# A gated delta-rule attention layer with a column-routed feed-forward: tile products in whole batches, and a new order of the work on all engines

## The chip, the cores and the metric

The kernel runs on one core of a Trainium2 chip. The time is the device time of one execution in microseconds; lower is better. The core has five engines that run side by side and meet at semaphores: PE (TensorE, matrix products, with PEld for its weight loads), DVE (VectorE), ACT (ScalarE), POOL (GpSimd) and SP (SyncE, which here issues the DMAs).

## The reference, cut to what matters

All is in fp32; x is 4 sequences of 2048 tokens of 512 numbers, 16 heads of 32.

```
q, k, v, gate = x@Wq.T, x@Wk.T, x@Wv.T, x@Wg.T      # heads of 32; x is layer-normed before
beta  = sigmoid(x@Wb.T)
alpha = exp(-exp(A_log) * softplus(x@Wa.T + dt_bias))
q = q/|q|/sqrt(32);  k = k/|k|
for each token t:                                   # S: 32x32 per sequence and head
    S = S*alpha_t
    delta = (v_t - k_t.S) * beta_t
    S = S + k_t (x) delta
    y_t = q_t.S
x1 = x + layernorm( (rmsnorm(y)*silu(gate)) @ Wo.T + bo )
xf = layernorm(x1)
logits = cos(xf, col_emb) + sigmoid(gelu(xf@gate_w1 + b1)@gate_w2 + b2)     # 16 columns
e = argmax(logits);  w = softmax(logits)[e]
out = x1 + layernorm( LN( (w*gelu(xf@W_cols[e] + b_cols[e])) @ proj_w[e] + proj_b + xf ) )
```

## The kernel before, in words

The recurrence is done in chunks of 32 tokens. A step handles a block of 64 tokens of all four sequences (256 tokens), in two chunks c = 0, 1. There are 32 blocks. Four stages of different blocks run side by side in one step, and `step` of each engine says with flags which of them are there: `ahead` (block b: norm, transposes, projections to q, k, gate, beta, v, decays), `chain` (block b-1: the recurrence), `after` (block b-2: output norm, output projection, residual, norm of x1, hidden layer of the gate), `late` (block b-3: logits, choice of the column, the scatter of rows by column). So there are 35 steps, 29 of them with all four stages. Behind them comes a second part over the columns' rows, which the change leaves as it is.

Each engine has one order of work, written out by hand in its `step`; an engine does its work in that order and waits in place. Heads lie as 16 groups g of 4 heads on the 128 partitions. What a head does alone is a product on a 32x32 tile of the array; `on_tiles(half, ...)` (lines 456 to 463) issues 8 groups times 4 heads of them. A batch is both halves, 64 products, which the trace shows as 128 records. They are, per chunk c:

- `key_products(c)` (L469): keys with keys and queries, into `kkq`
- `state_to_u(c)` (L477): keys with the state S, into `uk`
- `first_half_to_u(c)` (L485): the correction of a chunk's second half by its first
- `state_to_outputs(c)` (L492) and `chunk_to_outputs(c)` (L497): outputs, into `uq`
- `change_state(c)` (L504): into `su`, which `add_to_state` (DVE, L1165) adds to S

In the kernel before, most batches are issued in halves with large 128x128 products between them: `project` (L437, half of one projection, 8 records), `squares_sum` (L446), `output_projection` (L535), `gate_hidden` (L543), `gate_logits` (L553), `log_alpha` (L511), `decays` (L522) and the transposes `turn` (L454). Three PSUM banks (`work0` to `work2`) serve all these in the order of the list TURNS; `into` waits until the bank's last user was read.

DVE solves each chunk in two halves by forward substitution: `solve_half(c, j)` (L1145 to L1160), 15 rounds of four operations and a transpose. Its factors `pairs` are written to DRAM and fetched back by SP as rows broadcast over partitions (`write_rows`, `fetch_pairs`), and multiplied by beta on POOL (L992). ACT copies out of PSUM and evaluates functions; logarithm and exponential, sigmoid, and gelu lie in different tables, and a change of table is a table load in its stream. `token_norm` (L771 to L774) gives the scale of a layer norm, `norm_tokens` (L752) applies it, `length_of_normed` (L781 to L786) gives the length of the normed rows.

Of the kernel before, what the change touches and what calls it, by code (L numbers as in the profile page):

```python
# [16 lines left out]
H, DH = 16, 32  # L17
# [37 lines left out]
    ("logits",), ("xT", 0), ("xT", 1), ("qk", 0), ("rms", 0), ("rms", 1), ("alpha",), ("qk", 1), ("ss", 0),  # L55
    ("qk", 2), ("wo", 0), ("wo", 1), ("rank",), ("ss", 1), ("G", 0), ("G", 1), ("qk", 3), ("ss", 2),
    ("gate", 0), ("ss", 3), ("gate", 1), ("beta", 0), ("beta", 1), ("xfT", 0), ("xfT", 1), ("v", 0), ("v", 1),
    ("hid",),
]
BANK = {use: n % NW for n, use in enumerate(TURNS)}  # L60
READ_BY = dict(xT="xT_ready", qk="q_sq_ready", ss="ss_read", alpha="alpha_read", rms="rms_read", G="eg_ready", wo="wo_read",
               rank="rank_read", gate="gate_used", beta="beta_ready", v="v_read", xfT="xfT_ready", hid="h_ready",
# [26 lines left out]
def sandwich_kernel(nc, x, w_in, wa, dt_bias, a_log, norm_w, wo, bo, col_emb, gw1, gb1, gw2, gb2,  # L89
                    w_cols, b_cols, proj_w, proj_b, ln_g, ln_b,  # L90
                    c_sq, c_sel, c_mask, c_iota, c_pad, c_tok, c_row, c_col, out, xs_dram):
    with ExitStack() as ctx:
# [34 lines left out]
        minus_half = sb("minus_half", [P, 1])  # L127
# [17 lines left out]
        qraw = [sb(f"qraw{n}", [P, GU * T]) for n in range(2)]  # L145
        qsq = [sb(f"qsq{n}", [P, GU * T]) for n in range(2)]
        qr = [sb(f"qr{n}", [P, GU * T]) for n in range(2)]
        sg = sb("sg", [P, GU * T])
# [36 lines left out]
        gsb = qsq[1][:], ctx_flat[:, 0:GU * T]  # L185
        gT = qraw[1][:], ctx_flat[:, GU * T:2 * GU * T]
# [35 lines left out]
        def in_qr(*shape, dt=F32):  # L222
# [37 lines left out]
            v_full beta_full gate_full v_read beta_ready vb_free gate_ready gate_used  # L260
# [55 lines left out]
        def _(sp):  # L316
# [44 lines left out]
            def step(chain, after, ahead, block, following):  # L361
# [5 lines left out]
                if chain:  # L367
                    write_rows(1)
                    fetch_pairs(1, 0)
                    fetch_pairs(1, 1)  # L370
                if ahead:
                    load_tokens(following)
                    write_rows(0)
                if after:
                    store(block)
                if ahead:
                    fetch_pairs(0, 0)
# [41 lines left out]
        def _(pe):  # L419
# [45 lines left out]
            def key_products(c, half):  # L465

                if not half:
                    take(pe, "A_ready", free=1, use="kkq")
                on_tiles(half, "kkq_full", lambda g, q, q_half: pe.matmul(  # L469
                    kkq[q, g], kq[q, g, c, 0, :], kq[q, g, c].rearrange("p a t -> p (a t)"), start=True, stop=True))  # L470

            def state_to_u(c, half):

                if not half:
                    take(pe, "kqd_ready")
                    take(pe, "S_ready")
                on_tiles(half, "uk_full", lambda g, q, q_half: pe.matmul(  # L477
                    uk[q, g], S[q, g, :], kqd[c][q, g, 0, :], start=(g == 0), stop=True, skip_group_check=True))

            def first_half_to_u(c, half):  # L480

                if not half:
                    take(pe, "A_ready")
                    take(pe, "delT_ready")
                on_tiles(half, "corr_full", lambda g, q, q_half: pe.matmul(  # L485
                    uk[q, g, CS:C], delT[c][q_half, g, :], Ak[c][q_half, 1, g, :],
                    start=False, stop=True, skip_group_check=True))

            def state_to_outputs(c, half):
                if not half:  # L490
                    take(pe, "uq_free", free=1)
                on_tiles(half, None, lambda g, q, q_half: pe.matmul(  # L492
# [959 lines left out]
```

## Time and profile before

| | us |
|---|---|
| three runs | 3433.52 median (3429.26 to 3442.22) |
| profiled execution, its own time | 3454.87 |
| its span, first to last instruction | 3453.1 |
| mean granted TensorE clock, of full | 0.912 |
| the 35 steps, from the start to about | 3072 |
| ACT busy, of the span | 1824.4 |
| DVE busy | 2357.6 |
| POOL busy | 1913.1 |
| DMA, mean share of 16 engines | 0.42 + 0.05 + 0.01 by queue |

Busy time of one engine overlaps that of the others; matmul records overlap each other as well, so differences between starts are safer than durations. The second part over the columns takes the last 380 us or so of the span. An engine's idle time is shown with who ended it; "issue" is a wait for which the profile shows no releaser.

### The profile page before, as it was taken

How to read it: one execution, taken by the hardware profiler on the slowest of the kernel's cores; microseconds unless marked ns; L12 is line 12 of the kernel's file. 1: busy time of each engine (PE TensorE's matmuls, PEld its weight loads, DVE VectorE, ACT ScalarE, POOL GpSimd, SP SyncE). 2: the span in 40 equal slices, each digit the busy share in tenths (PEclk: the TensorE clock that was granted, in tenths of full speed). 3: DMA queues.
4: the chain of work that ended last, by engine and by line, in shares of the span. 5: the costliest groups of instructions: out<-in, count | busy, mean ns of one | idle time of the engine just before them, and what ended most of it. 6: DMA issues, size and time to landing. Idle time of an engine off the chain costs nothing.

```text
span 3453.1 us, 141658 instructions
## 1 busy us (share of the span) xinstructions
PE 3006.9 (87%) x59368; PEld 2295.4 (66%) x59368; DVE 2357.6 (68%) x10708; ACT 1824.4 (53%) x4154; POOL 1913.1 (55%) x2903
## 2 busy tenths in 40 slices
PE   4899999999999999999999999999999999637774
PEld 4667777777777777777777777777777777414443
DVE  1667666666666766777666666666666677657896
ACT  2355555555555555555555555555555555326664
POOL 1555565455555555555565555555556555416887
PEclk9899999999999999999999999999999999759997
DMA  3544444544444445444444454444445444545773
GB/s 112 132 119 115 113 117 112 124 117 108 118 115 114 117 121 124 112 113 117 115 117 112 124 124 110 114 115 115 116 116 124 124 111 118 142 141 105 132 126 65
DMA packets 350030, 404.87 MB, mean 117 GB/s; under 512 B 31169, under 2 KB 293953, under 8 KB 348881
## 3 DMA queue, kind: packets, MB, share of 16 engines
q1 hardware_dynamic: 332752, 362.10, 42.1%
q0 software_dynamic: 16640, 33.71, 5.4%
q8 instruction: 468, 7.67, 1.0%
q14 instruction: 170, 1.38, 0.1%
HBM read 323.97 MB, written 75.93 MB: 116 GB/s over the span
## 4 chain that ended last, share of the span: by engine, by line
PE 62%; ACT 20%; DVE 11%; issue 4%; POOL 1%; ACTq 1%; DMA 1%; POOLq 0%; SPq 0%; DVEq 0%
PE work L437 25%; PE work L535 7%; PE work L543 3%; PE work L446 3%; DVE uk L1158 3%; DVE Ut L1155 3%; PE su L504 3%; PE work L454 2%; PE uq L497 2%; PE uk L477 2%; PE kkq L469 2%; PE uq L492 2%; PE work L530 2%; PE work L522 2%; PE work L511 2%
## 5 line engine op out<-in xcount | busy, mean ns | idle before, releaser
L437 PE MATMUL work<-xT,w_sb 128*128 128x256 f32 x5120 | 1314.1, 407 | 6.5 <-ACT beta L835 5.1
L992 POOL TENSOR_TENSOR pairs<-pairs,beta 128x240 f32<-128x240 f32 (+14 forms) x1920 | 862.4, 488 | 667.0 <-ACT beta L835 380.9
L437 PEld LDWEIGHTS work<-xT,w_sb 128*128 128x128 f32 x5120 | 996.3, 202 | 183.8 <-issue 31.1
L1158 DVE TENSOR_TENSOR uk<-uk,Ut 128x120 f32<-128x120 f32 (+14 forms) x3840 | 708.6, 226 | 1.1
L1155 DVE TENSOR_TENSOR Ut<-pairs,uk 128x120 f32<-128x120 f32 (+14 forms) x3840 | 688.2, 215 | 5.5 <-POOL pairs L992 5.0
L802 ACT ACTIVATE qraw<-work 128x512 f32<-128x512 f32 x128 | 75.9, 593 | 432.2 <-DVE kq L1171 305.5
L1165 DVE TENSOR_TENSOR S<-Sd,su 128x512 f32<-128x512 f32 x64 | 44.0, 687 | 359.1 <-PE su L504 359.1
L535 PE MATMUL work<-wo_sb,ctxT 128*128 128x512 f32 x512 | 240.6, 613 | 6.3 <-POOL ctxT L1011 6.3
L1003 POOL TENSOR_TENSOR kd<-kd,dec 128x512 f32<-128x512 f32 x64 | 68.0, 1084 | 258.8 <-DVE kd L1237 258.8
L492 PEld LDWEIGHTS uq<-kqd,S 32*32 32x32 f32 x8192 | 90.7, 114 | 156.8 <-ACT oT L792 105.8
L1145 DVE TENSOR_TENSOR uk<-vT,uk 128x128 f32<-128x128 f32 x256 | 62.9, 291 | 187.7 <-PE uk L485 115.8
L492 PE MATMUL uq<-kqd,S 32*32 32x32 f32 x8192 | 105.6, 203 | 95.7 <-ACT oT L792 93.4
L809 ACT ACTIVATE qr<-work 128x512 f32<-128x512 f32 x128 | 75.9, 593 | 193.9 <-PE work L446 191.5
L1017 POOL TENSOR_TENSOR xfw<-xfw,pb_sb 128x1024 f32<-128x1024 f32 x32 | 75.5, 2359 | 175.7 <-DVE slot L1224 175.7
L535 PEld LDWEIGHTS work<-wo_sb,ctxT 128*128 128x128 f32 x512 | 93.7, 193 | 105.4 <-issue 94.8
L1171 DVE TENSOR_TENSOR kq<-qraw,qr 128x512 f32<-128x512 f32 x128 | 136.1, 1082 | 35.0 <-ACT qr L810 35.0
L839 ACT ACTIVATE vT<-work 128x512 f32<-128x512 f32 x64 | 38.2, 597 | 224.5 <-PE work L437 224.5
L981 POOL TENSOR_TENSOR kqd<-kq,eg 128x1024 f32<-128x1024 f32 x64 | 150.3, 2349 | 3.8 <-DVE kq L1171 3.8
L976 POOL TENSOR_TENSOR Sd<-S,eg_end 128x512 f32<-128x512 f32 x64 | 67.9, 1061 | 148.6 <-DVE S L1165 148.6
L446 PE MATMUL work<-qsq,squares 128*128 128x512 f32 x256 | 147.0, 658 | 0.0
L469 PEld LDWEIGHTS kkq<-kq 32*32 32x32 f32 x8192 | 119.1, 105 | 34.1 <-issue 29.8
L1194 DVE TENSOR_TENSOR lt<-work,gb_sb 128x32 f32<-128x32 f32 x32 | 6.1, 191 | 195.7 <-PE work L556 195.7
(249 smaller groups left out, 5970.8 us busy)
## 6 DMA issues: line engine op xcount, KB each, us to landing
pairs<-pair_rows SPq DMA_DIRECT2D x512, 256.0 KB, 3.5
pairs<-pair_rows SPq DMA_DIRECT2D x512, 224.0 KB, 3.7
xt<-in_x SPq DMA_DIRECT2D x66, 256.0 KB, 5.4
pair_rows<-Ak SPq DMA_DIRECT2D x64, 256.0 KB, 2.3
x<-in_x SPq DMA_DIRECT2D x64, 256.0 KB, 4.8
out<-x SPq DMA_DIRECT2D x64, 256.0 KB, 3.7
wo_sb<-xs_rows SPq DMA_DIRECT2D x30, 258.0 KB, 2.9
w_sb<-in_w_in SPq DMA_DIRECT2D x1, 5120.0 KB, 14.9
```

The source lines that it names most:

```text
L437: mm = pe.matmul(w[:, half * BT:(half + 1) * BT], w_sb[:, f, j * D + hg * P:j * D + (hg + 1) * P], xT[:, f, :], start=(f == 0), stop=(f == ...
L446: pe.matmul(w, blk1, qsq[n % 2][:], start=True, stop=True).then_inc(s["ss_full"], 1)
L469: on_tiles(half, "kkq_full", lambda g, q, q_half: pe.matmul(kkq[q, g], kq[q, g, c, 0, :], kq[q, g, c].rearrange("p a t -> p (a t)"), start ...
L492: on_tiles(half, None, lambda g, q, q_half: pe.matmul(uq[q, g], S[q, g, :], kqd[c][q, g, 1, :], start=(g == 0), stop=True, skip_group_chec ...
L504: on_tiles(half, "su_full", lambda g, q, q_half: pe.matmul(su[q, g, :], kd[c][q, g, :], delT[c][q, g, :], start=True, stop=True))
L535: mm = pe.matmul(w, flat(ctxT[:, hg * B + tb * BL:hg * B + (tb + 1) * BL, :]), wo_sb[:, hg, :], start=(hg == 0), stop=(hg == KD - 1))
L543: mm = pe.matmul(w[:, n * BT:(n + 1) * BT], gw1_sb[:, f, n * P:(n + 1) * P], xfT[:, f, :], start=(f == 0), stop=(f == KD - 1))
L981: link(nc.gpsimd.tensor_tensor(kqd[c][:], kq[:, :, c], eg[:, :, c * C:(c + 1) * C].unsqueeze(2).to_broadcast([P, G, 2, C]), ALU.mult), "kq ...
L992: ins = nc.gpsimd.tensor_tensor(a, a, beta[:, :, t:t + WID[t0]], ALU.mult)
L1155: link(v.tensor_tensor(Ut[:, g, 0:n], pr[:, g], uk[:, g, at:at + 1].to_broadcast([P, G // 2, n]), ALU.mult), "vb_free" if i and (c, j, t0) ...
L1158: link(v.tensor_tensor(uk[:, g, at + 1:at + 1 + n], uk[:, g, at + 1:at + 1 + n], Ut[:, g, 0:n], ALU.subtract), f"pairs_free{j}" if i and t ...
L1171: link(v.tensor_tensor(unit(kq, hp)[:, :, :, 1 - j, :], per_chunk(qraw[n % 2][:]), per_chunk(qr[n % 2][:]), ALU.mult), "kq_ready", hold=(n ...
```

## The change: what it does

- TensorE: `on_tiles` issues a whole batch, and the batches stand together where they did not: `state_to_u(0)`, `key_products(1)`, `state_to_outputs(0)` at the start of a step; `chunk_to_outputs(0)`, `state_to_u(1)`, `state_to_outputs(1)` behind `change_state(0)` and `output_projection(1)`; `first_half_to_u(1)` before `key_products(0)`. `change_state(1)` comes before two halves of v, `chunk_to_outputs(1)` and `gate_hidden`, in the step itself and not in the next one. TURNS has another order, and alpha's numbers share a bank with the logits.
- ScalarE: q and k are copied straight to `kq` (and scaled in place by DVE), the decays straight to `dec`. Sigmoid of beta is tanh and a linear step; the gate is copied, and its tanh is taken later; DVE's `gate_values` makes gate*(1+tanh(gate/2)), and the factor one half goes into `nw`. Both tanh come behind one table load with gelu, and `length_of_normed` moves to the next step. The output copy of chunk 0 stands before the norm of y, that of chunk 1 behind gelu.
- VectorE: another order; `output_rows` of both halves before `add_to_state`, the statistics of y behind the ranks; `decay_products(0)` inside `solve_half(1, 1)`; `vb_free` is signalled at that solve's start.
- GpSimd: decay differences before the scatter, `decay_state(1)` and the first part of `pairs_times_beta(1, 1)` before the residual sum.
- SP: `load_tokens` before `fetch_pairs(1, 1)`, `store` before `write_rows(0)`.

The diff's core:

```diff
-            def on_tiles(half, full, product):
-                for g in range(half * GU, (half + 1) * GU):
+            def on_tiles(product):
+                for g in range(G):
                     for h in range(HP):
                         mm = product(g, slice(DH * h, DH * h + DH), slice(DH * h, DH * h + CS))
-                if half and full:
-                    mm.then_inc(s[full], 1)
+                return mm
...
# TensorE, the new step
                 if chain:
+                    state_to_u(0)
+                    key_products(1)
+                    state_to_outputs(0)
                 if ahead:
                     take(pe, "xn_ready", TB)
                     turn("xT", xn, 0)
                     turn("xT", xn, 1)
                 if after:
                     outputs_squares_sum(0)
                     outputs_squares_sum(1)
                 if ahead:
                     take(pe, "xT_ready", 2)
                     project("qk", 0, 0, 0)
+                if late:
+                    gate_logits(0)
+                if ahead:
                     project("qk", 0, 0, 1)
+                if late:
+                    gate_logits(1)
+                if ahead:
+                    log_alpha(0, late)
+                    log_alpha(1, late)
                     project("qk", 0, 1, 0)
+                    project("qk", 0, 1, 1)
+                if chain:
+                    first_half_to_u(0)
+                if ahead:
                     squares_sum(0)
                     project("qk", 1, 0, 0)
                     project("qk", 1, 0, 1)
                     squares_sum(1)
                     take(pe, "lax_ready")
                     decays(0)
                     decays(1)
+                if after:
+                    take(pe, "ctx_ready", 2)
+                    output_projection(0)
+                if chain:
+                    change_state(0)
+                if after:
+                    output_projection(1)
+                if chain:
+                    chunk_to_outputs(0)
+                    state_to_u(1)
+                    state_to_outputs(1)
+                if late:
+                    ranks()
+                if ahead:
+                    squares_sum(2)
                     project("qk", 1, 1, 0)
                     project("qk", 1, 1, 1)
                     project("gate", 4, 0, 0)
+                    project("gate", 4, 0, 1)
                     squares_sum(3)
                     project("gate", 4, 1, 0)
                     project("gate", 4, 1, 1)
+                if chain:
+                    first_half_to_u(1)
+                if ahead:
                     take(pe, "kq_ready", 4)
+                    key_products(0)
                     project("beta", 3, 0, 0)
                     project("beta", 3, 0, 1)
                     project("beta", 3, 1, 0)
+                    project("beta", 3, 1, 1)
                 if after:
                     take(pe, "xf_ready", TB)
                     turn("xfT", xfw, 0)
                     turn("xfT", xfw, 1)
                 if ahead:
                     project("v", 2, 0, 0)
                     project("v", 2, 0, 1)
+                if chain:
+                    change_state(1)
+                if ahead:
                     project("v", 2, 1, 0)
+                    project("v", 2, 1, 1)
+                if chain:
+                    chunk_to_outputs(1)
                 if after:
                     take(pe, "xfT_ready", 2)
                     gate_hidden()
...
# ScalarE, new helpers and the new step's second half
+            def copy_gate(p, hp):
+                take(act, "gate_full")
+                link(nc.scalar.activation(flat(unit(silu[1 - p], hp)), bank("gate", hp), ACT.Copy), "gate_read", hold=True)
+            def gate_tanh(p, hp):
+                nc.scalar.activation(gate_t[hp], flat(unit(silu[1 - p], hp)), ACT.Tanh, scale=0.5).then_inc(s["gate_ready"], 1)
+            def beta_sigmoid(hp):
+                b = flat(unit(beta, hp))
+                take(act, "beta_full")
+                link(nc.scalar.activation(b, bank("beta", hp), ACT.Tanh, scale=0.5), "beta_read", hold=True)
+                link(nc.scalar.activation(b, b, ACT.Identity, scale=0.5, bias=half[:]), "beta_ready")
...
+                if after:
+                    take(act, "ctx_raw", 2)
+                if chain:
+                    copy_outputs(0)
+                if ahead:
+                    inverse_norm(2)
+                    copy_and_square(3)
                 if after:
                     take(act, "y_mv_ready")
                     token_norm(y_rn, y_mv)
                     norm_tokens(y, y, y_rn, "zn_ready")
                 if ahead:
                     pair_decays(0)
                     pair_decays(1)
+                    copy_gate(p, 0)
                     inverse_norm(3)
+                    copy_gate(p, 1)
                 if after:
                     take(act, "x1_mv_ready")
                     token_norm(x1_rn, x1_mv)
                     norm_tokens(xfw, x1, x1_rn, "xf_ready")
+                if ahead:
+                    take(act, "x_mv_ready")
+                    token_norm(x_rn, x_mv)
+                load_tanh_gelu()
                 if ahead:
                     if chain:
                         take(act, "vb_free")
+                        take(act, "pr_ready", 8)
+                    beta_sigmoid(0)
+                    beta_sigmoid(1)
+                    gate_tanh(p, 0)
+                    gate_tanh(p, 1)
...
# VectorE, the new step from the first correction on
                 if chain:
                     take(dve, "corr_full")
                     solve_half(0, 1)
+                if ahead:
+                    scale(0)
                 if late:
                     choose_columns()
+                if after:
+                    output_rows(0)
+                    output_rows(1)
+                if chain:
+                    add_to_state()
+                if ahead:
+                    for hp in range(2):
+                        take(dve, "g_copied")
+                        link(v.transpose(gT[hp], flat(unit(dec, hp))), "gT_ready")
                 if late:
                     weigh_columns()
                     rows_of_tokens()
+                if after:
+                    for tb in range(TB):
+                        token_stats(y, y_mv, tb, "y_mv_ready")
                 if ahead:
                     scale(1)
                 if chain:
                     take(dve, "uk_full")
                     solve_half(1, 0)
                 if ahead:
                     scale(2)
                     scale(3)
                 if after:
                     for tb in range(TB):
                         take(dve, "x1_ready")
                         token_stats(x1, x1_mv, tb, "x1_mv_ready")
                 if ahead:
+                    next_tokens_stats()
                     take(dve, "dec_ready", 2)
+                if chain:
+                    take(dve, "corr_full")
+                    solve_half(1, 1, {2: lambda: decay_products(0)} if ahead else {})
+                if ahead:
+                    gate_values(p, 0)
+                    gate_values(p, 1)
+                if chain:
+                    add_to_state()
```

## Rows read from the trace of the kernel before

**Rows 1.** The page: the span, TensorE's busy time, the queue that carries instructions.

```profile
span 3453.1 us, 141658 instructions
...
PE 3006.9 (87%) x59368; PEld 2295.4 (66%) x59368; DVE 2357.6 (68%) x10708; ACT 1824.4 (53%) x4154; POOL 1913.1 (55%) x2903
...
q8 instruction: 468, 7.67, 1.0%
```

**Rows 2.** TensorE in time: start, us, line, operation, records [idle before, who ended it].

```profile
56.32 5.34 PE L437 MATMUL work<-xT,w_sb 128*128 128x256 f32 x24
61.50 1.02 PE L446 MATMUL work<-qsq,squares 128*128 128x512 f32 x2
...
125.76 1.29 PE L504 MATMUL su<-delT,kd 32*32 32x32 f32 x128 [3.29 <-DVE delT L1160]
...
1408.99 0.75 PE L504 MATMUL su<-delT,kd 32*32 32x32 f32 x64
...
1435.91 1.99 PE L437 MATMUL work<-xT,w_sb 128*128 128x256 f32 x8
1437.84 1.10 PE L469 MATMUL kkq<-kq 32*32 32x64 f32 x64
...
1501.25 0.75 PE L504 MATMUL su<-delT,kd 32*32 32x32 f32 x64
```

**Rows 3.** TensorE's idle moments of one step; one row of the waits over the span.

```profile
1421.24 0.24 PE L477 MATMUL uk<-kqd,S 32*32 32x32 f32 x3 [0.35 <-issue]
1422.25 0.40 PE L477 MATMUL uk<-kqd,S 32*32 32x32 f32 x19 [0.76 <-issue]
...
1449.36 1.08 PE L492 MATMUL uq<-kqd,S 32*32 32x32 f32 x64 [2.94 <-ACT oT L792]
1451.90 1.12 PE L454 MATMUL work<-squares,xfw 128*128 128x128 f32 x4 [1.46 <-ACT beta L835]
...
1472.12 1.75 PE L454 MATMUL work<-squares,xn 128*128 128x128 f32 x8 [0.65 <-ACT xn L752]
...
PE uk L477 <- issue: 26.0, 52, 1.7
```

**Rows 4.** ScalarE in time, the same step.

```profile
1443.99 1.28 ACT L785 ACT_TABLE_LOAD   x1
...
1449.95 1.28 ACT L835 ACT_TABLE_LOAD   x1
...
1467.75 0.29 ACT L771 ACTIVATE nsc<-x_mv,eps 128x2 f32<-128x2 f32 x1
...
1470.55 1.52 ACT L752 ACTIVATE xn<-xt,x_rn 128x512 f32<-128x512 f32 x2
```

**Rows 5.** VectorE in time: a half solve's ends, a row of the ranks, scales, statistics.

```profile
1398.55 0.49 DVE L1145 TENSOR_TENSOR uk<-vT,uk 128x128 f32<-128x128 f32 x2 [1.27 <-PE uk L485]
...
1407.81 0.72 DVE L1160 STREAM_TRANSPOSE delT<-uk 128x512 f32<-128x512 f32 x1
...
1415.59 0.16 DVE L1219 TENSOR_TENSOR lt<-work,rows 128x32 f32<-128x32 f32 x1
...
1432.60 1.74 DVE L1171 TENSOR_TENSOR kq<-qraw,qr 128x512 f32<-128x512 f32 x2
...
1434.86 0.68 DVE L1121 BATCH_NORM_STATS2 stats<-x 128x6 f32<-128x512 f32 x1
```

**Rows 6.** Busy time by stretch, then granted clock, DMA share, GB/s; two projection rows.

```profile
1449.40:1456.00 6.60, 5.14 (x89) 4.15 (x93) 4.79 (x35) 2.90 (x4) 3.59 (x7) 0.55 0.72 139
1472.10:1476.00 3.90, 3.88 (x137) 3.49 (x138) 3.90 (x23) 1.51 (x4) 3.84 (x11) 0.56 0.18 40
1485.60:1489.80 4.20, 4.20 (x12) 2.80 (x11) 1.99 (x5) 0.69 (x3) 2.90 (x3) 0.59 0.71 130
...
1452.81 3.14 PE L437 MATMUL work<-xT,w_sb 128*128 128x256 f32 x8
...
1485.57 3.31 PE L437 MATMUL work<-xT,w_sb 128*128 128x256 f32 x8
```

More of the change, by code:

```diff
@@ L489, in state_to_outputs @@
[L489 to L492, printed above, removed]
-                    uq[q, g], S[q, g, :], kqd[c][q, g, 1, :], start=(g == 0), stop=True, skip_group_check=True))
-            def chunk_to_outputs(c, half):
-                on_tiles(half, "o_full", lambda g, q, q_half: pe.matmul(
-                    uq[q, g], delT[c][q, g, :], Aq[c][q, g, :], start=False, stop=True, skip_group_check=True))
@@ L500, in change_state, with key_products @@
-            def change_state(c, half):
-                if not half:
-                    take(pe, "delT_ready")
-                    take(pe, "kd_ready")
-                on_tiles(half, "su_full", lambda g, q, q_half: pe.matmul(
-                    su[q, g, :], kd[c][q, g, :], delT[c][q, g, :], start=True, stop=True))
-            def log_alpha(tb):
-                w = bank("alpha") if tb else into("alpha")
+                return mm
+            def key_products(c):
+                take(pe, "A_ready", free=1, use="kkq")
+                on_tiles(lambda g, q, q_half: pe.matmul(
+                    kkq[q, g], kq[q, g, c, 0, :], kq[q, g, c].rearrange("p a t -> p (a t)"), start=True, stop=True))\
+                    .then_inc(s["kkq_full"], 1)
@@ L510, in log_alpha, with change_state @@
+            def change_state(c):
+                take(pe, "delT_ready")
+                take(pe, "kd_ready")
+                on_tiles(lambda g, q, q_half: pe.matmul(
+                    su[q, g, :], kd[c][q, g, :], delT[c][q, g, :], start=True, stop=True)).then_inc(s["su_full"], 1)
+            def log_alpha(tb, late):
+                w = bank("alpha") if tb or late else into("alpha")
+                at = 2 * TB * E + tb * H
                 for f in range(KD):
-                    mm = pe.matmul(w[:, tb * H:(tb + 1) * H], xT[:, f, tb * P:(tb + 1) * P], wa_sb[:, f, :],
+                    mm = pe.matmul(w[:, at:at + H], xT[:, f, tb * P:(tb + 1) * P], wa_sb[:, f, :],
@@ L670, in step @@
                     turn("xfT", xfw, 0)
-                if ahead:
-                    project("beta", 3, 1, 1)
-                if chain:
-                    state_to_outputs(1, 0)
-                if after:
                     turn("xfT", xfw, 1)
@@ L1155, in solve_half @@
                         link(v.tensor_tensor(Ut[:, g, 0:n], pr[:, g], uk[:, g, at:at + 1].to_broadcast([P, G // 2, n]), ALU.mult),
[L1156 removed]
+                             behind=1)
                     for i, g in enumerate(turns):
@@ L1279, in step @@
                     scale(3)
-                    take(dve, "gate_ready")
-                    link(v.tensor_tensor(flat(unit(silu[1 - p], 0)), bank("gate", 0), sg[:], ALU.mult), "gate_used")
                 if after:
```

290 lines of the change are left out of this document (104 added, 186 removed).

## The prediction

> **What bounds the kernel now.** First the page's shares: TensorE is busy 87% of the span and leads the list; the reader is to see that nothing else comes near [rows 1]. Then TensorE's instructions in order of time, to find the period of the loop: the same batch of the state's change starts at 1408.99 and at 1501.25, so a step takes 92.26 us, and 32 such steps make about 2950 of the 3453 us [rows 2]. The kernel's time is therefore the step's time, and the step is read from TensorE: what it works on, where it stands idle, and where its clock is low.
>
> Idle in this step: 0.35 + 0.76 (inside state_to_u(1), no releaser shown), 2.94 (state_to_outputs(1) for ScalarE's copy of uq), 1.46 (xfT for the bank that beta's sigmoid reads) and 0.65 us (xT for xn), together 6.16 us [rows 3]. The two long ones have one cause in ScalarE's order: between 1435.6 and 1451.9 it runs the norm of x1, the length of the normed rows and the sigmoid in one string, with five table loads of 1.28 us in it, two of them shown [rows 4], while TensorE waits behind that string.
>
> Low clock in this step: three stretches of 6.6, 3.9 and 4.2 us with a granted mean of 0.55, 0.56 and 0.59, the rest at 1.0 (2.4 GHz); as the mean of a stretch mixes the two levels, twice what is missing to 1.0 makes 12.7 us at the lower one, 1.2 GHz [rows 6]. In them a projection half takes 3.14 and 3.31 us against 1.99 [rows 2, 6]; adding the same differences for the transposes and tile batches that lie there gives about 4.3 us lost. The first stretch follows the long idle time; the other two follow stretches of tile batches and narrow products with hardly an idle moment.
>
> So a step is 92.26 = 6.16 idle + 4.3 low clock + 81.8 of TensorE work at full clock.
>
> **The change part by part.**
>
> 1. Whole batches. A half batch of 32x32 products takes 0.75 us, a whole one 1.29, both with the same overlap of some 0.06 into the next row (1435.91 + 1.99 against 1437.84) [rows 2]. So a half costs 0.54, and each entry into tiles 0.15. The large products around pay too: a projection half among its like takes (61.50 - 56.32)/3 = 1.73 us, between tile batches 1.93, so 0.20 per group of tiles [rows 2]. I take 0.33 a group (both together, rounded down). Before, a full step has 22 groups of tiles separated by large products; after, 7: state_to_u(0) with key_products(1) and state_to_outputs(0); the first correction; the first state's change; chunk_to_outputs(0) with state_to_u(1) and state_to_outputs(1); the second correction with key_products(0); the second state's change; chunk_to_outputs(1). 15 fewer at 0.33 are -4.95 us. The arithmetic is unchanged. Ends: if only the switch inside the tiles counts, -2.2; if the large products' whole 0.20 counts, -5.3.
>
> 2. ScalarE's tables. Sigmoid becomes tanh with a linear step, in one set with gelu; the length of the normed rows moves to the next step's front, where logarithm and exponential are loaded. Eight loads a step become two, if tanh lies in gelu's set; if not, one more. At 1.28 us a load, six are 7.7 us of ScalarE, and two copies of the gate and two linear steps for beta (0.6 each, as the copies there) are 2.4 back. ScalarE has slack, so only its strings count. The Trainium skill (ScalarE: Activation LUTs, What ACT_TABLE_LOAD costs) gives about 2.66 us for a switch of set, 1.38 of it a drain after the load. The trace disagrees: the load at 1443.99 is followed at once by the next operations. By the page ScalarE would be freed of 16 us instead of 7.7; the sum here would be the same, since what is left of its strings is short.
>
> 3. The old idle times. The output copy stands now early in ScalarE's order, before y's norm: the 2.94 goes. 1.46 and 0.65 change their form and are counted anew below. So -6.16, and everything that is late next is added.
>
> 4. What is late next: a walk through the new order with the durations of rows 2, 4 and 5 at full clock, from state_to_u(0) at 0.
> - xn: gelu, the output copy, one table load and norm_tokens (1.52 [rows 4]) end at about 4.4; the three tile batches end at 4.1. 0.3 to 0.4.
> - solve(0,1) takes 9.97 us (1398.55 to the end of the transpose at 1408.53 [rows 5]) and starts at 20.8; the state's change comes at 31. No wait, but nothing to spare.
> - The product between the state's change and the next chunk: add_to_state now stands behind output_rows(1), which needs output_projection(1). It ends at 36.0, S is there at 37.5, and chunk_to_outputs(0) covers 36.0 to 37.2. 0.3.
> - The second correction: after ranks TensorE has six projection halves and two sums of squares, 12.2 us; VectorE has in the same time five small operations (0.16 to 0.2 each), statistics of y (two at 0.68 and an aggregate of 0.2 each), one scale (0.87) and solve(1,0) (9.97), 13.5 us [rows 5]. Wait 1.3 to 1.4.
> - key_products(0) needs scale(2) and (3), 1.74 us after that solve [rows 5], with a correction of 1.2 in between: 0.5.
> - xfT's second turn needs the bank read by beta's tanh: statistics of x1 and of the next tokens 3.5, x1's norm 2.8 + 1.5 (1467.75 to the end of 1470.55's two), the tokens' norm 2.8, a load 1.28 and the tanh 0.6 stand against key_products and beta's four halves: 1.4. Then v waits 0.5 for the second tanh.
> - solve(1,1), with decay_products in it, ends at 71.3; the state's change comes at 72. After it come v's last two halves, chunk_to_outputs(1) and gate_hidden, 8.5 us, which cover S for the next step.
> Sum 4.3 us of new waits (rounding included). Everything queued behind such a wait on TensorE is delayed with it, and ScalarE and VectorE follow.
> GpSimd and the queue of SP: fetch_pairs(1,1) is now behind load_tokens, which waits for eg; the walk has its data 3 us or more before GpSimd reaches them, and the other three fetches earlier still. This is hidden; if the cover went, it would cost what the fetch is late, 1 to 3 us. Waits on the buffers (kd, kqd, kt, gate_used) are added, all satisfied 2 us or more before. Bounds of the new waits: 0.8 (only those without chain) to 8.
>
> 5. Supply of instructions. The idle moments with no releaser are 26.0 us in 52 times at state_to_u over the span, the longest 1.7 [rows 3]; all instructions come by a queue of 7.67 MB [rows 1]. They fall in a stretch of tiles. I keep them at 1.4 a step with longer stretches of tiles (bounds 0 to 5).
>
> 6. Clock. The two low stretches that follow narrow work stay; the one after the long idle time should shrink, but three tile batches in a row are new. I take 3.8 us of loss instead of 4.3 (bounds 0.5 to 12).
>
> Sum: 81.8 - 4.95 + 4.3 + 1.4 + 3.8 = 86.35 us a step, 5.9 less. Times 31 (thirty full steps and two partial ones) -183, and 5 less at the closing steps, where table loads of x1's norm lie on the path. The profiled execution took 3454.87 us and would take 3267; the median of the three runs is 21 below it, so 3433.5 - 188 = **3245 us**. The later part over the columns isn't touched.
>
> **The rivals.**
> - A, the clock stays up: loss 0.5 instead of 3.8, a step of 83.05, 3433.5 - 286 - 5 = 3143. For it: the longest idle time left is 1.4 us. Against: two of three low stretches came without idle time.
> - B, tiles in a row outrun their instructions: each of the three long groups of tiles stalls by 1.4 instead of one, +2.8, a step of 89.2, 3334. For it: the stalls lie in tiles, and with up to 192 small products in a row there has been no row. Against: a batch of 128 records ran in 1.29 at 125.76 without one.
> - C, slower: the low clock takes over. Place: the groups of three batches at the step's start and in its middle, each with waits near it (xn, S, the second correction). Price: 3.31 against 1.99 is 0.4 to 0.45 us per us at the lower level. It decides from about 22 us low in a step (granted mean under 0.88 against 0.93), where the loss reaches 9.7 and eats the 5.9; at 28 us a step is 95, 3433.5 + 85 = about 3520. The Trainium skill (TensorE: Matmul & The Clock Gate, A second HAM failure mode) says that frequent short idle moments between groups of products bring the clock down again and again; that would speak for C. The trace bears it out in part only: the stalls of 0.35 and 0.76 left the clock at 1.0, the 2.94 did not.
> - D, no change: the new waits reach their bound of 8 and B's stalls come on top, +6.5 on the forecast, a step of 92.85, 3433.5 + 18 - 5 = 3447, within 17 us of before. For it: the walk has several places with nothing to spare. Against: both must come at once.
>
> **How the numbers follow.** The forecast has 0.64 (its own range 3190 to 3300), A 0.12, B 0.10, C 0.10, D 0.04. 0.5% of 3433 is 17 us, about what a measurement can tell from none. Faster: forecast, A and B, 0.86; the same 0.04; slower 0.10. The range reaches from A's time to a little over B's, 3140 to 3350, and leaves out C and D and the tail beyond A.
>
> **What would show it.** A step's period near 86 with 7 groups of tiles at 1.2 to 1.3 us a batch and projection halves at 1.73 (1); two table loads a step (2); no idle at state_to_outputs(1) for ScalarE (3); idle before first_half_to_u(1), xfT and v of 1 to 1.5 us, VectorE or ScalarE named (4); idle without releaser inside the long groups (5, B); the granted clock by stretches (6, A, C). It is wrong if one of the new waits is over 4 us, if the step's granted mean leaves 0.90 to 0.96, or if a batch in a row takes over 1.5 us.

## The result, and the profile after

The changed kernel takes 3638.5 us (median of 4 runs, 3623.8 to 3656.2) against 3435.9 for the kernel before in the same comparison: a ratio of 1.059, 95% interval 1.054 to 1.065. It is slower by 203 us; the forecast was 3245.

The page after, the same lines as in [rows 1], and the granted clock by slices:

```profile
span 3641.3 us, 141487 instructions
...
PE 2997.7 (82%) x59368; PEld 2372.4 (65%) x59368; DVE 2353.2 (65%) x10710; ACT 1654.4 (45%) x4103; POOL 1912.2 (53%) x2903
...
PEclk9889889889988889898898898889988998668898
...
q8 instruction: 468, 7.67, 0.9%
```

TensorE has the same number of records and nearly the same busy time, and a longer span: it waits more. For whom, its waits over the span say (engine, line, waited for: us, times, longest):

```profile
PE uq L488 <- issue: 138.5, 64, 4.4
PE kkq L465 <- issue: 122.9, 59, 3.4
PE uk L473 <- issue: 88.7, 39, 4.1
```

All three large ones have no releaser (I call such a wait a stall), and nearly all of them stand at the second and third batch of a group: state_to_outputs, key_products, state_to_u. The engines' waits that the prediction walked through are nearly gone.

Counting over whole steps makes the comparison exact. Stretches of whole steps, from one ranks product to another of a later step (columns as in [rows 6]), before:

```profile
486.65:2796.70 2310.05, 2156.02 (x45509) 1669.21 (x45501) 1593.35 (x7877) 1262.52 (x2800) 1291.23 (x1950) 0.93 0.47 117
```

and after:

```profile
421.39:2778.06 2356.67, 2056.64 (x43685) 1656.60 (x43680) 1524.40 (x7560) 1071.34 (x2640) 1238.90 (x1872) 0.89 0.44 110
```

The first holds 25 steps, the second 24: a step takes 92.40 and 98.19 us. With TensorE's idle time in the same stretches from its waits, and the low clock as twice what the granted mean lacks to 1.0. The mean is printed with two digits, so each time at the low clock is known to about 1 us here; added up over 300 short windows it is 13.2 before and 22.0 after. The work is not measured: 76.85 is the forecast's own figure, and the loss is what it leaves over:

| a step, us | before | forecast | after |
|---|---|---|---|
| work at full clock (worked out) | 81.8 | 76.85 | 76.85 |
| stalls without releaser | 1.13 | 1.4 | 12.05 |
| waits for other engines | 5.02 | 4.3 | 0.45 |
| what is left: loss at the low clock | 4.4 | 3.8 | 8.8 |
| sum | 92.4 | 86.35 | 98.2 |
| of it, time at the low clock | 12.9 | | 21.6 |

8.8 of loss on 21.6 us is 0.41 us for each at the low clock, which fits the two projection halves of [rows 6] (3.31 against 1.99 us: 0.40); so the forecast's work for the kernel after stands, as an estimate. Before, 4.4 on 12.9 is only 0.34; at 0.40 the work there would be about 81.0, 0.8 less than the prediction took.

TensorE in time in the kernel after, the group of three at a step's start and the one in its middle (columns as in [rows 2]):

```profile
1548.55 0.83 PE L473 MATMUL uk<-kqd,S 32*32 32x32 f32 x76 [0.19 <-issue]
...
1549.23 0.91 PE L465 MATMUL kkq<-kq 32*32 32x64 f32 x48
1552.02 1.26 PE L465 MATMUL kkq<-kq 32*32 32x64 f32 x75 [1.87 <-issue]
...
1555.49 0.98 PE L488 MATMUL uq<-kqd,S 32*32 32x32 f32 x78 [1.71 <-issue]
...
1582.29 1.29 PE L501 MATMUL su<-delT,kd 32*32 32x32 f32 x128
...
1590.93 0.94 PE L473 MATMUL uk<-kqd,S 32*32 32x32 f32 x90 [1.55 <-issue]
...
1594.40 1.49 PE L488 MATMUL uq<-kqd,S 32*32 32x32 f32 x92 [2.17 <-issue]
```

Two things are to be seen. The stalls are in the middle of a batch, where no semaphore is waited for. And they stand 3.47 us apart (1548.55, 1552.02, 1555.49; 1590.93, 1594.40), with 128 records between them: 92 of state_to_u and 36 of state_to_outputs in the last pair (rows of one to three records, where two batches overlap, are left out above). The instruction queue tells what 128 records are. 7.67 MB for 2 x 59368 records (a product and its weight load each) is 64.6 bytes an instruction, so queue q8 carries TensorE's instructions and hardly any others, and 7.67 MB in 468 packets is 16.4 KB a packet. A packet then holds about 254 to 256 instructions: 128 records with their weight loads, exactly one batch of tiles.

What the stalls bring with them, by stretch behind the group in the middle (granted clock is the third number from the right):

```profile
1588.00:1592.00 4.00, 2.00 (x212) 1.80 (x198) 2.62 (x7) 0.60 (x1) 2.49 (x3) 1.00 0.54 119
1592.00:1596.00 4.00, 1.83 (x117) 1.65 (x104) 0.00 (x0) 0.00 (x0) 2.52 (x3) 0.55 0.50 139
1596.00:1600.00 4.00, 4.00 (x12) 2.88 (x13) 2.01 (x8) 0.30 (x1) 1.18 (x1) 0.50 0.59 131
```

TensorE is idle half of the first 8 us, and the granted clock falls from 1.00 to 0.50 for the ranks and the projections behind.

ScalarE's tables came as meant. The table loads in the whole program after, two a step and one for the second part, are 36 + 35 + 1; before, there were 251, eight in a full step:

```profile
L712 ACT ACT_TABLE_LOAD x36 | 46.2, 1283 | 31.1 <-DMA nw<-in_norm_w 30.4
L715 ACT ACT_TABLE_LOAD x35 | 44.9, 1283 | 0.7
L919 ACT ACT_TABLE_LOAD x1 | 1.3, 1283 | 0.0
```

### The profile page after: what moved, and what is told of

It reads as the page before. It is cut to its first block, busy times and chain, and to the rows that moved or that the text cites. A ratio compares the mean times of both kernels' runs of the same rounds, so it can differ in the third digit from the quotient of the medians.

```text
span 3641.3 us, 141487 instructions
## 1 busy us (share of the span) xinstructions
PE 2997.7 (82%) x59368; PEld 2372.4 (65%) x59368; DVE 2353.2 (65%) x10710; ACT 1654.4 (45%) x4103; POOL 1912.2 (53%) x2903
## 3 DMA queue, kind: packets, MB, share of 16 engines
q8 instruction: 468, 7.67, 0.9%
## 4 chain that ended last, share of the span: by engine, by line
PE 73%; issue 12%; DVE 8%; ACT 4%; POOL 1%; ACTq 1%; DMA 0%; DVEq 0%; POOLq 0%
PE work L435 30%; PE work L533 6%; PE kkq L465 4%; PE work L444 4%; PE work L541 3%; PE uq L488 3%; PE uk L473 2%; PE work L528 2%; PE work L452 2%; PE su L501 2%; PE uk L481 2%; PE uq L493 2%; PE work L509 2%; PE work L520 2%; PE work L551 1%
## 5 line engine op out<-in xcount | busy, mean ns | idle before, releaser
L435 PE MATMUL work<-xT,w_sb 128*128 128x256 f32 x5120 | 1254.4, 402 | 6.6 <-ACT beta L814 3.3
L435 PEld LDWEIGHTS work<-xT,w_sb 128*128 128x128 f32 x5120 | 1029.4, 204 | 243.9 <-issue 88.9
L465 PE MATMUL kkq<-kq 32*32 32x64 f32 x8192 | 175.2, 243 | 128.6 <-issue 122.9
L1007 POOL TENSOR_TENSOR dec<-dec,xn 128x512 f32<-128x512 f32 x64 | 81.8, 1278 | 326.5 <-DVE xn L1262 326.5
L465 PEld LDWEIGHTS kkq<-kq 32*32 32x32 f32 x8192 | 154.0, 123 | 140.5 <-issue 134.3
L488 PEld LDWEIGHTS uq<-kqd,S 32*32 32x32 f32 x8192 | 114.1, 134 | 143.8 <-issue 143.8
L770 ACT ACTIVATE kq<-work 128x512 f32<-128x512 f32 x128 | 75.8, 592 | 230.9 <-PE work L435 230.8
L473 PE MATMUL uk<-kqd,S 32*32 32x32 f32 x8192 | 95.4, 198 | 96.3 <-issue 88.7
L473 PEld LDWEIGHTS uk<-kqd,S 32*32 32x32 f32 x8192 | 84.4, 109 | 111.8 <-issue 111.4
L995 POOL COPY xt<-la 128x1024 f32<-128x1024 f32 x32 | 33.2, 1036 | 221.7 <-DVE la L1173 221.7
```

The lines of the kernel that those rows point to most:

```text
L435: mm = pe.matmul(w[:, half * BT:(half + 1) * BT], w_sb[:, f, j * D + hg * P:j * D + (hg + 1) * P], xT[:, f, :], start=(f == 0), stop=(f == ...
L465: on_tiles(lambda g, q, q_half: pe.matmul(kkq[q, g], kq[q, g, c, 0, :], kq[q, g, c].rearrange("p a t -> p (a t)"), start=True, stop=True))\
L473: on_tiles(lambda g, q, q_half: pe.matmul(uk[q, g], S[q, g, :], kqd[c][q, g, 0, :], start=(g == 0), stop=True, skip_group_check=True))\
L488: on_tiles(lambda g, q, q_half: pe.matmul(uq[q, g], S[q, g, :], kqd[c][q, g, 1, :], start=(g == 0), stop=True, skip_group_check=True))
L1007: link(nc.gpsimd.tensor_tensor(d, d, gT[hp], ALU.subtract))
```

## The experiments

Theory S, formed on the trace after: TensorE's instructions arrive in blocks of one batch at a pace of their own, and batches in a row outrun it. Rivals: W, the new order's own waits; T, tile products in a row are slow by themselves. All experiments give the reference's arithmetic but where the text says otherwise.

**e1_apart.** The kernel after, TensorE's `step` alone reordered so that no two batches stand together. In short form, with | between the parts (xT the transposes of xn, rms `outputs_squares_sum`, ss `squares_sum`, and qk, gate, beta halves of those projections):

```diff
-state_to_u(0) key_products(1) state_to_outputs(0) | xT | rms | qk
+state_to_u(0) | xT | key_products(1) | rms | qk | state_to_outputs(0)
-chunk_to_outputs(0) state_to_u(1) state_to_outputs(1) | ranks | ss 2 | qk, qk | gate
+chunk_to_outputs(0) | ranks | ss 2 | state_to_u(1) | qk, qk | state_to_outputs(1) | gate
-first_half_to_u(1) key_products(0) | beta
+first_half_to_u(1) | beta | key_products(0)
```

> The kernel after, with TensorE's order changed alone: whole batches stay, but no two stand side by side; key_products(1) behind the xT transposes, state_to_outputs(0) behind a projection half, state_to_u(1) behind ranks and a sum of squares, state_to_outputs(1) behind two projection halves, key_products(0) behind a half of beta. 12 groups of one batch instead of 7. Theory S (supply): TensorE's instructions come in blocks of 7.67 MB / 468 = 16.4 KB, 256 instructions of 64 bytes, as many as one batch has (128 products and 128 weight loads); a batch eats one in 1.3 us and the next isn't there. With large products between, the stalls without releaser, 11.9 us a step in the kernel after, fall to 1 to 3 us; a step of 98.1 goes to 87 to 90, 3290 to 3380 in all. Theory W (waits of the new order, VectorE's solves behind output_rows and ranks): stays at 97 to 99 a step, 3600 to 3650. Theory T (a change of kind of tile product, PSUM target or operand costs it, whatever stands between): every batch stalls still, no gain, 3600 or more.

Measured: 3375.9 us, ratio to before 0.982 (0.979 to 0.985). So 262 us, more than the whole slowdown, are undone by TensorE's order alone, and W and T fall. A step takes 89.58: stalls 3.14, waits for other engines 4.62, 7.2 us at the low clock. The waits:

```profile
PE work L452 <- ACT xn L726: 67.9, 25, 3.0
PE uk L473 <- issue: 36.7, 33, 2.3
PE uk L481 <- DVE delT L1156: 20.3, 17, 2.6
PE work L452 <- ACT beta L820: 16.5, 15, 2.2
```

The largest, 2.7 us a step for xn, belongs to e1's order and not to the forecast's walk:

```profile
2502.39 1.29 PE L473 MATMUL uk<-kqd,S 32*32 32x32 f32 x128
2506.71 1.97 PE L452 MATMUL work<-squares,xn 128*128 128x128 f32 x8 [3.04 <-ACT xn L726]
```

The transposes start 4.32 us after state_to_u(0), and the forecast had xn ready at 4.4; but e1 has one batch of 1.29 us in front of them, where the kernel after has three. In the kernel after xn is ready 4.27 us after state_to_u(0) (1551.99 on ScalarE) and the transposes come at 1556.40, since the stalls hold TensorE up that long. The other waits of e1 make 1.9 us a step, where the walk had 3.9.

**e4_front.** e1 with the first group in a row again.

> As e1, but with the first group of the kernel after kept: state_to_u(0), key_products(1), state_to_outputs(0) in a row at the step's start; everything else apart. Theory S: this group alone stalls 3.5 us a step as it does in the kernel after (1.9 and 1.7 in a step), and saves two switches: +2.8 to +3.5 us a step over e1, +90 to +110 in all, and the stalls stand inside the group's second and third batch, about 128 records after each other. Theory W: no difference from e1.

Measured: 3414.0 us, ratio 0.994 (0.992 to 0.996), 38 us over e1, where 90 to 110 was expected. Stalls rise from 3.14 to 7.02 a step, somewhat more than expected, but waits fall from 4.62 to 1.77: the stalls, and the two batches now there, stand in front of the wait for xn and take its place. The step is only 1.6 longer. A stall costs nothing where there would be a wait anyway.

**e2_halves.** The kernel after with every batch cut in halves, large products between.

> The kernel after, with TensorE's order changed alone: every batch is issued in two halves with a large product or transposes between, 21 to 22 groups a step as in the kernel before, all other engines as in the kernel after. Theory S: no stalls beyond the 1 to 1.5 us a step of the kernel before; against e1 it pays the switch in and out of tiles ten times more, 0.33 each, +3.3 us a step, +100 in all minus what e1 still stalls: 3350 to 3450. Theory W: as e1, no gain over the kernel after, 3600 or more. If the switch costs nothing, it is equal to e1 or faster.

Measured: 3576.5 us, ratio 1.043 (1.040 to 1.045). Stalls are 0.43 a step, fewer than anywhere, as S says. But the time is outside S's 3350 to 3450, and by the time alone W (3600 or more) is nearer; it is 200 over e1 where 100 was expected. A step is 95.88, 6.3 more than e1's: 2.7 less of stalls, 3.1 more of waits for other engines (7.73, most of it for VectorE's delT and ScalarE's xn; likely since the second halves stand behind more products, which no run takes apart), and 5.9 of work and low clock. By the short windows it has 7.2 us more at the low clock (14.0 against 6.9), about 2.9 at 0.40 each, so about 3.0 is left for nine or ten more groups of tiles, 0.3 each (an estimate).

**e3_before_whole.** The kernel before, each batch whole at its first half's place:

```diff
-                for g in range(half * GU, (half + 1) * GU):
+                if half:
+                    return
+                for g in range(G):
...
-                if half and full:
+                if full:
```

> The kernel before, with one edit: each batch is issued whole where its first half stood; the second half's place is empty. 12 groups instead of 22, none side by side. If whole batches save 0.33 each and single ones don't stall: -3.3 us a step, about -100, 3335. Theory S: small stalls may come where a batch meets few large products (chunk_to_outputs, one projection, key_products), up to 2 us a step, then -40 to -100. Theory T or a loss from whole batches as such: slower than before, 3450 to 3550.

Measured: 3418.0 us, ratio 0.995 (0.993 to 0.997). The gain is there, but it is 17 us, a sixth of what the switches promised and outside the 40 to 100 expected. A step is 90.83, 1.57 shorter: stalls 1.22 as before, waits 5.74 (+0.7), and 15.6 us at the low clock instead of 13.2 by the short windows, about 1 us of loss at 0.40. Ten groups fewer at 0.33 are -3.3, and the sum comes out at -1.5.

**e5_rows and e6_rows_traffic.** The kernel before with rows of products on constants ahead of its first step; in e6 with 80 transfers of 256 KB beside them, two at a time. In short form:

```diff
+            tiles(6, C, n32);  large(24)       # 6 batches in a row, 32 columns
+            tiles(6, 2 * C, n64);  large(24)   # 64 columns
+            tiles(6, P, n128);  large(24)      # 128 columns
+            for _ in range(6):
+                tiles(1, C, n32);  large(4)    # one batch, one projection half
+            for _ in range(6):
+                tiles(1, C, n32);  large(8)    # one batch, two halves
```

> The kernel before, with a stretch of products put ahead of its first step, whose results nobody reads, and no transfer running meanwhile: 6 batches of 32x32 products in a row with 32 columns; 6 with 64; 6 with 128; then 6 single batches of 32 columns with 4 large products (one projection half, 1.73 us) between; then 6 with 8 (3.46 us) between; 24 or 16 large products between these parts. Theory S: after one to three batches at 1.2 us the row runs at the pace of the blocks of instructions, one batch in 2.5 to 3.5 us, the same for 32 and 64 columns, with pauses each 128 records; single batches with one half between (3.0 us) run with small pauses or none, those with two (4.7 us) with none. Theory T (tiles slow by themselves in a row): pauses don't come each 128 records, and 64 columns take longer than 32 by their columns. If the supply suffers from transfers alone: no pause here at all.

> As e5, while the queue of SP runs 80 broadcast transfers of 256 KB, two outstanding, as for the pairs. If the blocks of instructions wait behind other transfers in the DMA engines: the pace of a row of batches goes from that of e5 to 3.5 us or more a batch. If the pace is the queue's own: the same as in e5 within 0.3 us.

TensorE in time in e5, no transfer running:

```profile
43.33 1.74 PE L710 MATMUL uk<-squares 32*32 32x32 f32 x183
47.49 1.27 PE L710 MATMUL uk<-squares 32*32 32x32 f32 x128 [2.43 <-issue]
51.23 1.93 PE L710 MATMUL uk<-squares 32*32 32x32 f32 x128 [2.46 <-issue]
...
80.59 1.99 PE L710 MATMUL kkq<-squares 32*32 32x64 f32 x128 [1.44 <-issue]
84.04 1.99 PE L710 MATMUL kkq<-squares 32*32 32x64 f32 x128 [1.47 <-issue]
...
103.72 16.57 PE L710 MATMUL work<-squares 32*32 32x128 f32 x599
120.58 5.11 PE L710 MATMUL work<-squares 32*32 32x128 f32 x169 [0.28 <-issue]
...
139.32 0.45 PE L710 MATMUL uk<-squares 32*32 32x32 f32 x31
140.03 1.02 PE L710 MATMUL uk<-squares 32*32 32x32 f32 x97 [0.27 <-issue]
...
175.66 1.29 PE L710 MATMUL uk<-squares 32*32 32x32 f32 x128
176.88 3.72 PE L715 MATMUL work<-w_sb 128*128 128x256 f32 x16
180.53 1.29 PE L710 MATMUL uk<-squares 32*32 32x32 f32 x128
```

Here is the cost by itself. In a row a batch comes each 3.73 us with 32 columns and each 3.45 to 3.73 with 64, with a pause at each 128 records, though 64 columns are twice as many: the pace is the instructions'. Meanwhile the core moves 4 GB/s (from 43 to 66 us), what one packet of 16.4 KB each 3.73 us makes (4.4), so the blocks are all that moves. A limit on single instructions would spread the pauses; here 128 records run through in 1.3 to 2 us and then the row stands still. The row starts with 183 records before its first pause, so what lay ready and came meanwhile is one block and a part. With 128 columns a batch is work for 3.5 us, and the one pause is 0.28. One batch with one projection half (1.73 us) between has pauses of 0.27 to 1.77 us; with two halves (3.46 us) none. T is refuted. Without transfers a batch of 1.29 us wants more than 1.73 us of other work, and 3.46 is enough; by the pace it would be about 2.4 (3.73 less 1.29, an estimate). S's own range for the pace, 2.5 to 3.5 us, was a little low.

The same row with transfers (e6):

```profile
50.73 1.93 PE L719 MATMUL uk<-squares 32*32 32x32 f32 x128 [3.94 <-issue]
55.56 1.93 PE L719 MATMUL uk<-squares 32*32 32x32 f32 x128 [2.91 <-issue]
61.75 1.93 PE L719 MATMUL uk<-squares 32*32 32x32 f32 x128 [4.27 <-issue]
```

The pace goes to 4.8 to 6.2 us a batch (the core moves about 195 GB/s, more than the 110 to 117 of the kernels' steps): the blocks come later beside other transfers. Here two halves between are not always enough either: the last batches pause for 0.18 to 1.27 us inside.

**e7_little_traffic.** The kernel after, each fetch of pairs cut to one row, so that its solves work on other numbers:

```diff
-rows = pair_rows[c, j, h, j * CS + PARTS[n]:j * CS + PARTS[n + 1], 0:G * CS]
+rows = pair_rows[c, j, h, j * CS + PARTS[n]:j * CS + PARTS[n] + 1, 0:G * CS]
...
```

> The kernel after, with each fetch of pairs cut to one row per part (the other rows of pairs stay what they were, so the solves work on other numbers; all instructions of the engines stay), 1/15 of the bytes. If the stalls come from transfers: 11.9 us of stalls a step fall to 3 or less, a step at 87 to 89, 3300. If the blocks have a pace of their own: stalls fall by at most 2 to 4 us, 3530 to 3640.

Measured: one run of 3570 us. The core moves 41 GB/s in the steps instead of 110, and stalls fall only from 12.05 to 10.00 us a step, the step from 98.19 to 95.35. So in the kernel after most of the stall is there with little traffic too, and about 2 us goes with the traffic; it is one run.

**e8_xn_early.** e1, and ScalarE's `norm_tokens(xn)` of the next step before `take(act, "hid_full")`.

> e1, and ScalarE normalizes the next step's tokens (xn) before it waits for gate_hidden, not after gelu, the output copy and a table load. In e1 TensorE waits for xn 2.95 us a step, the largest wait. Theory S (walk): the 2.5 to 3 us go, up to 1 comes back as a stall of instructions, since key_products(1) then follows state_to_u(0) earlier: -1.5 to -2.5 us a step, -45 to -80 on e1's 3376: 3295 to 3330. Rival: the wait is only passed on to the first correction, where VectorE's solve ends: then within 20 of e1.

Measured: 3315.2 us, ratio 0.968 (0.964 to 0.973), by the ratios 47 us less than e1. Waits fall from 4.62 to 1.63, stalls rise from 3.14 to 4.60: half of the wait comes back as a stall, 1.5 us where up to 1 was expected. The time is in the expected range.

**e9_spaced, e10_mid_joined, e11_four_halved.** e8 with TensorE's batches spread by what e5 showed; the same with the middle group in a row; e9 with four batches in halves. In the short form of e1:

```diff
# e9 against e8
+... rms | qk | key_products(1) | logits, qk, logits, alpha | state_to_outputs(0) | qk, qk ...
+... chunk_to_outputs(0) | ranks | ss 2 | qk | state_to_u(1) | qk | gate | state_to_outputs(1) ...
+... first_half_to_u(1) | beta, beta | key_products(0) ...
# e10 against e9
+... chunk_to_outputs(0) state_to_u(1) state_to_outputs(1) | ranks | ss 2 | qk, qk | gate ...
# e11 against e9: key_products(1), state_to_outputs(0), (1), chunk_to_outputs(1) in halves
```

> e8, and TensorE's batches spread by the pace that e5 and e6 showed (a block of instructions, one batch, in 3.5 us without other transfers, 4.0 to 6.2 with): key_products(1) and state_to_outputs(0) later behind more large products, state_to_u(1) one projection half later, state_to_outputs(1) and key_products(0) two halves behind the batch before. Theory S: the stalls, 4.5 us a step in e8, fall to 1.5 to 3: -1.5 to -3 us a step, 3220 to 3270. Rival D (VectorE): state_to_u(1) one half later moves solve(1,0) and with it the second correction, whose wait takes all of it back: within 20 of e8's 3315.

> e9, with the group chunk_to_outputs(0), state_to_u(1), state_to_outputs(1) in a row as in the kernel after. Theory S: two blocks late inside it, 1.55 and 2.17 us in a step of the kernel after: +3 to +3.7 us a step over e9 less two switches (0.66): +75 to +100. If only the last of a group's wait counts since others hide behind it (as the group in front of the step did in e4, +38): +30 to +50.

> e9, with four batches that nothing urgent waits for (key_products(1), state_to_outputs(0) and (1), chunk_to_outputs(1)) cut in halves with a large product between: 16 groups of tiles instead of 12, no other change. If a switch into and out of tiles costs 0.33: +1.3 us a step, +41 in all; up to 0.5 of it comes back where halves thin out the stream of instructions: +25 to +41. If the switch is free: 0 or faster.

Measured, on a chip where the kernel before took 3455: e9 3353.2, ratio 0.970 (0.967 to 0.973); e10 3510.0, 1.015 (1.012 to 1.019); e11 3388.5, 0.981 (0.980 to 0.983). By ratios:

- e9 doesn't beat e8 (their intervals overlap), where 45 to 95 us were expected. Stalls fall from 4.60 to 2.65, and waits rise from 1.63 to 3.44: 1.15 more for beta's tanh and 0.95 for the squares of the outputs, both ScalarE's, and 0.3 less for VectorE. The exchange is nearly one for one, as the rival said, though behind another engine than it named. And half of the stalls that are left in e9 are of another kind, a wait of about 0.5 us, then two or three records, then another:

```profile
1558.45 0.59 PE L488 MATMUL uq<-kqd,S 32*32 32x32 f32 x40
1559.56 0.22 PE L488 MATMUL uq<-kqd,S 32*32 32x32 f32 x2 [0.52 <-issue]
1560.30 0.99 PE L488 MATMUL uq<-kqd,S 32*32 32x32 f32 x86 [0.52 <-issue]
```

  Such pairs stand in the kernel before, in e9 and in e11 (1.3 us a step in e9), and in no other run. The supply in blocks of 128 records doesn't explain them, and no run here tells what does.
- e10 is 0.045 over e9, 155 us where 75 to 100 was expected. Its step is 94.24 against 88.57: stalls 6.01 against 2.65, +3.4, as expected, waits 0.4 less, and 2.7 more of work and low clock. As two switches are saved (0.7), the low clock takes about 3.3, with 17.0 us low in a step against 7.1. Its trace in time shows both, and the last line is e9 in the same part of a step:

```profile
1538.83 0.94 PE L473 MATMUL uk<-kqd,S 32*32 32x32 f32 x90 [2.53 <-issue]
...
1543.12 1.49 PE L488 MATMUL uq<-kqd,S 32*32 32x32 f32 x92 [2.87 <-issue]
...
1548.12 8.01 PE L435 MATMUL work<-xT,w_sb 128*128 128x256 f32 x32
...
1544.00:1552.00 8.00, 8.00 (x67) 6.31 (x58) 5.25 (x19) 1.23 (x2) 3.88 (x3) 0.62 0.35 76
...
1548.00:1556.00 8.00, 7.09 (x240) 5.76 (x227) 7.66 (x17) 1.82 (x3) 6.10 (x5) 1.00 0.54 130
```

  Four projection halves take 7.8 us behind the stalls, where they take 6.9 to 7.0 at full clock, and ranks and the sum of squares before them 1.5 to 1.9 times their time at full clock.
- e11 is 0.0112 over e9, 38 us for four more groups of tiles; 41 was the most expected. The intervals reach 0.002 to 0.003 to each side. In the traces a step is 0.82 longer: stalls 0.65 more, waits 1.2 less, work and low clock 1.36 more, of which about 0.35 is the clock. So a switch into and out of tiles costs 0.25 to 0.3 us.

## Why the prediction was wrong, by its own steps

- **Part 1, whole batches:** the mechanism and the size hold, as an estimate. Whole batches take 1.29, and e11 has the switch at 0.25 to 0.3. With 0.40 us lost for each at the low clock, the work left in a step is 82.1 in e2 (21 to 22 groups of tiles), 80.7 in e11 (16), 79.1 to 79.7 in e1, e8 and e9 (12) and 76.9 in the kernel after (7): 0.35 a group, and five microseconds for all.
- **Part 2, tables:** right, two loads a step, and the time of one is 1.283 as before.
- **Part 3, old idle times:** right for uq's wait, which is gone in e1 too; xfT's comes back at 0.66 us a step in e1, where Part 4 had 1.4.
- **Part 4, what is late next:** 4.3 was forecast, and 0.45 came in the kernel after, where the stalls covered the rest. That e1 has 4.62 is luck: 2.7 of it is the wait for xn that e1's own order makes (the walk's time for xn, 4.4, was right), and the others are 1.9 where 3.9 was forecast.
- **Part 5, supply of instructions, is the step that failed:** "I keep them at 1.4 a step with longer stretches of tiles (bounds 0 to 5)". It was 12.05. Of the 11.8 us by which the step missed, 10.65 is here and 5.0 in the clock, less 3.85 of waits that were covered. The term was carried over from the kernel before without a reason for its size. Its stalls were no measure of it: at state_to_u they are mostly pairs such as [rows 3] shows, 0.35 and 0.76 with three records between, of which the kernel after has none. The block could have been read from [rows 1], in packets of 16.4 KB, and with it that a single batch, as the one of 1.29 us in [rows 2], runs on one block and could not speak against rival B. The pace of 3.5 us a block stood in no row.
- **Part 6, the clock:** 3.8 was forecast and 8.8 came, at 21.6 us low a step. Rival C had it decide at about 22 us low and named the groups of three as the place. It was not the cause by itself: e10 against e9 shows the low clock coming with the stalls (3.4 us more of stalls, about 3.3 us more of loss), and e1, without the groups, has 7.2 us low.
- **The rivals:** what happened is B's mechanism at four times B's price (10.65 instead of 2.8 over the forecast) and C's on top of it. Treated as separate, each was too small: B was to leave the kernel faster. In these runs they come as one chain: behind the stalls of the middle group the granted clock goes from 1.00 to 0.50, and in e9, without the group, it stays at 1.00 there.

What stays open: why the clock fell more in e3, where neither stalls nor waits grew much; and what makes the pairs of stalls two to four records apart. That blocks are fetched one after another, or with one in reserve, is read from the pace and from the 183 records before the first pause, not seen in the transfers themselves.

## What to carry to other kernels

Count the instructions of a dense stretch, not only its time: here TensorE is supplied with one block of 256 instructions in about 3.5 us, and more slowly beside transfers, so small products must be mixed with so much large work that each 256 instructions last at least 3.5 us. Batches may be whole (a switch is about 0.3 us), but not in a row. Spreading them further pays only until another engine's wait takes the stall's place, as in e9. And price a stall together with the clock that it takes down: 3.4 us of stalls made e10's step 5.7 longer, 1.7 times as much. The order with whole batches apart and xn's norm early, e8, is 3.2% faster than the kernel before.

## What the runs showed of the hardware that had not been expected

- The supply: 3.45 to 3.73 us for 128 fp32 matmul records with their weight loads, with 32 columns or 64, and 4.8 to 6.2 us with 32 columns beside transfers at 195 GB/s (e5, e6); in the kernel after, 3.47 us between stalls.
- "issue" in the waits, a wait without releaser in the middle of a batch, is this supply where it comes back after 128 records. Waits without that period don't follow from it: the pairs of e9 are about 0.7 us apart, with two records between, and their cause is open.
- A stall can take a wait's place: e4 has 3.9 us more stalls than e1 and a step of 1.6 more.
